# Attention steps: the next rows' low parts ahead of the gating's rows, and the gating's transposes inside the next step's projections

## The reference, cut to what matters

```python
h = tok(x)                                # 64 images -> 64 * 37 rows of 192
# attention with relative positions, 8 heads, on the normalized rows
xn = layernorm(h)
q, k, v = xn @ Wq * K**-0.5, xn @ Wk, xn @ Wv
content = einsum('bhtk,bhsk->bhts', q + r_w_bias, k)
rel = relative_shift(einsum('bhtk,rhk->bhtr', q + r_r_bias, pos_emb @ Wrk))
h = h + (softmax(content + rel) @ v) @ Wo + bo
# mixture of 8 experts: the gate, the two best, a capacity by priority, two products per expert
xf = layernorm(h)
logits = xf @ Wg                          # 192 -> 8
topv, topi = top_k(logits, 2);  w = softmax(topv)
h = h + experts(xf, topi, w)
```

## Time and profile before

| | us |
|---|---|
| median of three runs | 622.51 |
| the profiled execution, its own time | 623.27 |
| its span, first to last instruction | 621.5 |
| PE busy | 539.1 (87%) |
| DVE busy | 431.6 (69%) |
| ACT busy | 258.7 (42%) |
| POOL busy | 222.0 (36%) |
| mean granted TensorE clock | 0.939 |

### The profile page before, as it was taken

How to read it: one execution, slowest core, us unless ns; L and a number is a source line. 1 busy time by engine, 2 the same in 40 slices (tenths; PEclk the granted TensorE clock), 3 DMA queues, 4 the chain that set the end, 5 groups by cost and what they waited for, 6 DMA issues and landing times.

```text
span 621.5 us, 12359 instructions
## 1 busy us (share of the span) xinstructions
PE 539.1 (87%) x4284; PEld 501.0 (81%) x4284; DVE 431.6 (69%) x1002; ACT 258.7 (42%) x412; POOL 222.0 (36%) x206
## 2 busy tenths in 40 slices
PE   5989428999999999999999796667999999999982
PEld 4988428989999899899899683344899999999982
DVE  6828764776776777777767757672778777777753
ACT  1322403542443434425425204402865685595560
POOL 0137711012021021120120205017587788776463
PEclk9998759999999999999999857869999999999997
DMA  8799663202102112012022008504275476476160
GB/s 200 166 223 225 196 132 60 51 2 51 40 11 50 28 22 50 17 34 50 6 45 44 8 1 219 150 1 133 81 164 134 94 165 139 93 144 150 19 166 30
DMA packets 61497, 55.84 MB, mean 90 GB/s; under 512 B 28693, under 2 KB 52053, under 8 KB 60671
## 3 DMA queue, kind: packets, MB, share of 16 engines
q1 hardware_dynamic: 52319, 46.92, 30.4%
q0 software_dynamic: 9152, 8.59, 8.4%
HBM read 40.21 MB, written 18.27 MB: 94 GB/s over the span
## 4 chain that ended last, share of the span: by engine, by line
PE 45%; DVE 14%; ACT 13%; issue 10%; SPq 5%; DMA 5%; POOL 4%; DVEq 2%; POOLq 1%; ACTq 0%
PE PS L1018 7%; PE PS L741 6%; PE PS L718 6%; PE PS L697 5%; ACT wide L1055 4%; PE PS L1016 4%; ACT hTh L1197 3%; DMA wide<-x 2%; PE PS L734 2%; PE PS L732 2%; PE PS L733 2%; PE PS L725 2%; DVE hTl L1657 2%; PE PS L993 2%; SPq L472 2%
## 5 line engine op out<-in xcount | busy, mean ns | idle before, releaser
L1708 POOL TENSOR_TENSOR rs<-ve,nhalf 111x1 f32<-111x1 f32 (+2 forms) x37 | 24.5, 662 | 270.0 <-DVE ve L1345 195.0
L1839 POOL DMA_INDIRECT running_sums<-ye,gid x42 | 74.8, 1780 | 33.5 <-DVE ye L1681 24.3
L1018 PE MATMUL PS<-w2hl,hTh 128*128 128x384 f32 (+1 forms) x288 | 82.8, 357 | 0.0
L1016 PE MATMUL PS<-w2hl,hTl 128*128 128x192 f32 (+1 forms) x288 | 73.6, 255 | 4.2 <-DVE hTl L1657 4.0
L1813 POOL DMA_INDIRECT xe<-routed_rows,gid x48 | 53.1, 1107 | 42.8 <-DVE gid L1622 28.6
L993 PE MATMUL PS<-xeT,w1h 128*128 128x370 f32 x288 | 64.2, 331 | 2.1 <-issue 1.4
L1657 DVE TENSOR_TENSOR hTl<-hf,hTh 128x740 fp32r<-128x740 f32 x48 | 44.6, 929 | 24.6 <-ACT hTh L1197 23.1
L1016 PEld LDWEIGHTS PS<-w2hl,hTl 128*128 128x128 f32 (+1 forms) x288 | 53.7, 186 | 6.8 <-issue 5.6
L1018 PEld LDWEIGHTS PS<-w2hl,hTh 128*128 128x128 f32 (+1 forms) x288 | 52.9, 184 | 0.5
L993 PEld LDWEIGHTS PS<-xeT,w1h 128*128 128x128 f32 x288 | 50.4, 188 | 2.8 <-issue 1.8
L697 PE MATMUL PS<-xT,wh 128*128 128x222 f32 x264 | 47.3, 289 | 5.5 <-DVE xT L1359 5.5
(11 more groups left out here) (240 smaller groups left out, 1286.1 us busy)
## 6 DMA issues: line engine op xcount, KB each, us to landing
wide<-x SPq DMA_DIRECT2D x12, 576.0 KB, 13.7
w1r<-L_ffn_W SPq DMA_DIRECT2D x16, 384.0 KB, 4.8
rel_scores<-wide SPq DMA_DIRECT2D x66, 73.0 KB
w2r<-L_ffn_W SPq DMA_DIRECT2D x8, 576.0 KB, 4.4
w1r<-L_ffn_W SPq DMA_DIRECT2D x16, 192.0 KB, 4.5
wide<-rel_scores SPq DMA_DIRECT2D x22, 111.0 KB, 2.3
out<-running_sums SPq DMA_DIRECT2D x1, 1776.0 KB, 8.0
narrow<-L_tok_pos_embedding SPq DMA_DIRECT2D x6, 288.0 KB
```

Source lines behind the costliest of these rows:

```text
L1016: pe.matmul(PS[0:n, bank, 0:D], hTl[:, c, at], w2hl[:, c, 0, :], start=(c == 0), stop=False, skip_group_check=True)
L1018: last = pe.matmul(PS[0:n, bank, 0:2 * D], hTh[:, c, at], both(w2hl[:, c, :, :]), start=False, stop=(c == HC - 1), skip_group_check=True)
L1839: p_.indirect_dma_start(sums, at, ye[0:r, e % 2, n, :], None, bounds_check=B * T + NT * 128 - 1, oob_is_err=True, compute_op=ALU.add).then ...
```

## The change

Three edits, in the lists of PE, ACT and DVE.

The diff:

```diff
--- before.py
+++ after.py
@@ -787,18 +787,19 @@
                 project(0, 0, 1, s_qp)
                 project(0, H * K, 2, s_kp)
                 if before2:
-                    gate(s - 2)
-                if before2:
+                    gate_rows(s - 2)
                     pe.wait_ge(s_h1[0], s - 1)
                 project(1, 0, 0, s_qp)
+                if before2:
+                    gate(s - 2)
+                if before_:
+                    pe.wait_ge(s_p[0], s)
+                    probs_transposed(0)
                 if before2:
                     pe.wait_ge(s_l, s - 1)
                 elif before_:
                     pe.wait_ge(s_v[1], s)
                 project(1, H * K, 3, s_kp)
-                if before_:
-                    pe.wait_ge(s_p[0], s)
-                    probs_transposed(0)
                 pe.wait_ge(s_qr, s + 1)
                 if before_:
                     pe.wait_ge(s_sc[1], s)
@@ -842,12 +843,11 @@
                 else:
                     pe.wait_ge(s_re[0], 1)
                 content(1)
-                if before_:
-                    gate_rows(s - 1)
 
             def last_step():
 
                 s = STEPS - 1
+                gate_rows(s - 1)
                 pe.wait_ge(s_h1[0], s)
                 gate(s - 1)
                 pe.wait_ge(s_p[0], s + 1)
@@ -1125,6 +1126,8 @@
             def step(s):
 
                 before_ = not is_step(s, 0)
+                if before_ and not is_step(s, 1):
+                    gate_rows(s - 2)
                 if before_:
                     probs(s - 1, 0)
                 if before_ and not is_step(s, 1):
@@ -1419,6 +1420,9 @@
                     ch(v.bn_stats(st2[:, :], h_all[:, 2 * s + g, :]))
                     ch(v.bn_aggr(mv2[:, g, :], st2[:, :]))
                     v.tensor_scalar(ve2[:, g:g + 1], mv2[:, g, 1:2], EPS, None, ALU.add).then_inc(s_vb[g], 1)
+
+            def normed_rows(s):
+
                 for g in range(2):
                     dve.wait_ge(s_rb[g], s + 1)
                     if g == 0:
@@ -1444,6 +1448,8 @@
                 if before_:
                     residual(s - 1)
                 rows_low(s + 1)
+                if before_:
+                    normed_rows(s - 1)
 
             col = lambda a, at: bc(a[:, at].rearrange("p (g a) -> p g a", a=1), [G, at.stop - at.start, E])
             lanes = lambda which, at: bc(iota8[:, which:which + 1, :], [G, at.stop - at.start, E])
@@ -1520,6 +1526,7 @@
                                 part(oTh).bitcast(F32), ALU.subtract).then_inc(s_ot[1], 1)
                 choice_weights(0, before)
                 residual(s)
+                normed_rows(s)
                 member_prios(before)
                 dve.wait_ge(s_mp, 1)
                 for a, z in REPEATS_DVE:
```

## The result

The changed kernel took **631.0 us** in the median of 20 executions (622.44 to 645.6), the kernel before 622.93 in 20 beside it (621.5 to 624.57). The ratio is 1.0059 [1.0036, 1.0082]; it comes from executions within 1.5% of each kernel's fastest alone, and since this kernel spreads by 3.7% by itself, it says less than the medians, which are 1.3% apart. A second set of nine gave 631.14 (624.71 to 635.39), ratio 1.0099 [1.0068, 1.0130]. The forecast was 623.8, in 620.6 to 625.6: the time lies outside the range, on the slow side.

A forecast was written before the change was run, and what follows sets the result against it. A pass was taken as bound by the chain from the output product over DVE's low parts, PE's projections and ACT's in-order list to the second `probs`; 9 x 0.18 less 0.37 on the median 622.51 gave 623.8, range 620.6 to 625.6.

The forecast's parts named there:

- The pass: Each of nine attention-loop passes (steps 2 to 10): 0.18 us longer, bounds 0.04 to 0.36, though PE's projections start 0.97 earlier.
- the four transposes: The gate's transposes on PE, now between k(0) and q(1): 0.40 us, formerly done in a stretch of waiting.
- q(1): PE's second query projection, ahead of the gate: taken as half of the twenty matmuls, 1.12 us.
- `probs` of group 0: ACT's first exponential in a pass: start at about 230.45, from a softmax on DVE some 0.35 us earlier.
- The last step: Step without projections, DVE's softmax on the path: it starts about 0.37 us earlier, so -0.37.
- The sum of 1.25: Whole kernel: nine passes at 0.18 make 1.62, less 0.37 in the last step, +1.25 us.
- The queries held: ACT's list: `logits` waits for the gate to 231.75, with all eight queries and the second `probs` behind; chance 0.79.
- PE's gain is kept: Rival: queries not held, so PE gains 0.57 us a pass and 0.37, 5.5 in all: 617.0; chance 0.12, partial gain included.
- the longer wait on PE: PE's wait ahead of the second transposed probabilities grows from 0.31 to about 1.1 us in each pass.
- the clock in the loop: Rival: PE's longer wait drops its clock to 1.2 GHz, up to 15 us more a pass: 630 or more; chance 0.03.
- The sign of being wrong: In the profile after: granted clock below 1.00 in the loop; others named were no idle ahead of `logits`, passes below 24.2.
- The clock of the last step: Rival: a shorter gap keeps PE at 2.4 GHz there, some 6 us saved, 617.5 with the sum; chance 0.06.

The follow-up runs named there:

- the second profile: Another profiled execution of the changed kernel, nothing edited: 635.39 us, span 633.6; that set of nine had a median of 631.14.
- the first profile: The first profiled execution of the changed kernel: 623.79 us, span 622.0, one of the nine executions between 622.44 and 625.47.
- the one with 1140 columns: Kernel before with a ScalarE copy of 1140 columns that nothing reads ahead of the second `probs` in steps 2 to 10: 669.01 us, ratio 1.0748.

## Why the prediction was wrong

**The pass: right, to within 0.07.** With 0.40 taken off, PE's projections start at 227.04 (forecast 227.04), the gate ends at 231.74 (231.75), `logits` starts at 231.88 (231.87), the first query at 231.98 (231.99), the second `probs` at 234.62 (234.61), and PE goes on at 235.74 (235.72) behind a wait of 1.09 (about 1.1). Two terms were off against each other: the four transposes take 0.31 to the next matmul (0.40) and q(1) 1.20 (1.12). The 1.12 doesn't follow from its own sentence: half of the 2.33 for twenty matmuls is 1.17. And `probs` of group 0 starts at 230.38 (230.45) for another reason than was given: DVE's softmax comes 0.58 earlier (227.41 against 227.99), not 0.35, and `probs` is held by the copy of `xnT` ahead of it on ACT. That it came out is luck, and it cost nothing, since `logits` waits longer.

The passes behind the loop's first wait grew by 0.13 (24.43 against 24.30), not by 0.18: PE goes on 0.20 later, and 0.07 of it lies in the 0.40. DVE's last statistic, before and after:

```profile
225.93 0.15 DVE L1421 TENSOR_SCALAR ve<-mv 111x1 f32<-111x1 f32 x1
```

```profile
226.40 0.15 DVE L1422 TENSOR_SCALAR ve<-mv 111x1 f32<-111x1 f32 x1
```

The subtraction follows it by 0.07, where the normalizing followed by 0.14. The forecast put the one in the place of the other. The first of the nine passes grew by 0.40. DVE stands idle for 0.23 where it enters the loop; that now comes ahead of the low parts, and in the kernel before it came ahead of the gate's rows, in place of the wait for POOL. PE's two ends of this pass, before and after:

```profile
114.13 1.03 PE L712 MATMUL PS<-ident,wide 111*111 111x111 f32 x8 [0.58 <-ACT wide L1079]
138.36 1.03 PE L712 MATMUL PS<-ident,wide 111*111 111x111 f32 x8 [0.31 <-ACT wide L1079]
```

```profile
113.80 1.03 PE L712 MATMUL PS<-ident,wide 111*111 111x111 f32 x8 [0.43 <-ACT wide L1079]
138.43 1.03 PE L712 MATMUL PS<-ident,wide 111*111 111x111 f32 x8 [1.10 <-ACT wide L1079]
```

**The last step: right in sign.** From the last pass's wait to DVE's masking it was 22.70 us (332.74 to 355.44) and is 22.21 (333.84 to 356.05), so -0.49 against -0.37. Together 0.40 + 8 x 0.13 - 0.49 = +0.95. The profiled executions differ by 0.52, since the changed one came to step 1 0.3 earlier (its second transposes start at 113.80 against 114.13), and the kernels with the wait filled by 1.1 and 1.3. The sum of 1.25 stands for the order by itself. Its bounds, added to 622.51, make 622.5 to 625.4, not 622.4 to 625.3, and the range goes to 625.6 where its upper bound is 625.4; 631.0 lies outside either way.

**The queries held: borne out.** ACT stood idle for 0.55 ahead of `logits`, and all eight queries came behind it. This agrees with the Trainium skill ("PSUM — Partial Sum Buffer", section "Engine vs sequencer instructions"), by which ScalarE's queue is strictly first in, first out. The rival "PE's gain is kept" needed queries that aren't held, and gave 5.5 less. With the copy moved out of their way the kernel takes 616.69, 6.5 less than the 623.15 of before beside it, and a pass is 0.64 shorter (0.57 in the rival): the condition was right, and it was the list's order that failed it.

**The step that failed: the longer wait on PE was costed at nothing.** The text said that PE's 0.97 "ends as a longer wait ahead of the second transposes" and priced only the period. The rival with the right mechanism, the clock in the loop, had "630 or more" and a chance of 0.03. Its counter-argument was the granted clock of 1.00 in the loop "with as much waiting in two pieces". The two pieces, 0.44 and 0.31, make 0.75, which isn't as much, and the sum counts the wrong thing: with two waits of 1.48 in sum 1 execution in 11 strayed, with 1.32, of which 1.09 in one place, 20 of 29. PE's waits in the loop of before went up to 0.44, and behind a stretch of 2 us without work the clock was at 0.50; a wait of 1.1 lay between a row for either side, and 0.03 gave nearly all to the one. The rival's price for a pass was too high, up to 15 us more, so that a single one would come to 630. The runs showed 3.3 to 4.8, since the clock came back before the pass was over (from 220.75 on in the pass shown). That makes 628 or 629 with one such pass; by these prices (an estimate) the median of 631 takes about two. The sign of being wrong that the prediction named, a granted clock below 1.00 in the loop, is what came.

The Trainium skill's page was drawn on for one sentence alone ("TensorE: Matmul & The Clock Gate", section "What's actually happening"), as if a loop in which PE is busy for most of the time were safe. Another section of it, "A second HAM failure mode: psum-queue depth-cycling", says that frequent small idle times between groups of matmuls make the clock swing between its two levels. That speaks against this change, and the changed kernel agrees: 1.00 and 0.50 in turn in the second profile, with one wait of 1.09 in each pass.

**The clock of the last step** fell in the changed kernel too: 0.54 over 353 to 371.5 in the first profile, against 0.50. From DVE's masking to the end of the span it takes as long as before to about 0.1 us (from 356.05 of 622.0, then from 355.44 of 621.5). Nothing of that rival came.

**What stays open**: why one pass with a wait of 1.09 is followed by a fall and the next isn't, and what else of the pass bears on it. Here only the wait's length was varied, at one place, with the same work behind it, and the two profiles with falls are all that shows the passes one by one.

## What to carry to other kernels

An engine that is brought forward gains nothing while a small instruction that depends on it stands ahead of independent work in another engine's list: move that instruction in the same edit (here a copy of 0.17 us decided between 631 and 616.7). When a change turns several short waits of TensorE into one long one, price the clock as well as the period, and look for spread: a median far above the fastest execution and one undisturbed profile can belong to the same kernel. If the wait can't be removed, a few products that nothing reads, put into it, keep the clock (two of them took 631 to 624.3).

## What the runs showed of the hardware

- In the loop the clock did not fall at the wait but after it, when PE was back at work: 0.5 to 2.2 us behind the wait's end over the eleven falls of two profiles (211.77 to about 213.95 in the changed kernel, 223.71 to about 225.0 in the one with 1140 columns). It then stayed at 1.2 GHz for 6.8 or some 10 us, with PE busy throughout. In the last step of the kernel before it fell inside the wait: 0.57 over 351 to 353, with no work on PE.
- The step is steep: 0.04 us of wait a pass, 1.05 against 1.09, is between 1 of 11 executions and two of three. At 1.34 eight of nine waits in one profile are followed by a fall.
- The values' 32 matmuls of 96 columns take 3.36 us at 2.4 GHz and 6.29 at 1.2 GHz (266.39 in the second profile), 1.9 times.
